# Value and phase projections in 128x32 tiles instead of 128x64, with a planner whose durations, restart and weights are set anew

## The reference

```python
for l in range(6):                                  # batch 4, 512 tokens, window of 126 keys
    q, k, v = x @ Wq.T + bq, keys @ Wk.T + bk, keys @ Wv.T + bv     # keys: a zero row, then x
    o = softmax(mask(q k.T / sqrt(8))) v @ Wo.T + bo                # 16 heads of 8
    x = ln(x + o);  x = ln(x + gelu(x @ W1.T) @ W2.T)               # 512 hidden
# block 2: token-shift mix: sigmoid(xr Wr) * (relu(xk Wk)^2 Wv)
# block 3: causal attention, with a gate for each head and key:
ph = x @ w_phase;  phase = arctan2(ph[..., 0], ph[..., 1])
gate = lock * exp((cos(phase - carrier) - 1) / bandwidth) + (1 - lock)
attn = softmax(causal(q k.T / sqrt(8) + log(gate + 1e-6)));  y = (attn v) @ wo
# block 4: a router picks 3 of 8 experts for each batch row; tanh-gelu feed-forward of 512 in each
```

## Time and profile before

| | us |
|---|---|
| median of 3 runs | 1088.59 |
| lowest, highest | 1084.31, 1092.73 |
| the profiled execution's own time | 1091.71 |
| its span in the trace | 1089.9 |
| PE busy in it | 992.6 (91%) |
| DVE, ACT, POOL busy | 803.6, 743.7, 394.4 |

### The profile page before, as it was taken

How to read it: one execution, slowest core, us unless ns; L and a number is a source line. 1 busy time by engine, 2 the same in 40 slices (tenths; PEclk the granted TensorE clock), 3 DMA queues, 4 the chain that set the end, 5 groups by cost and what they waited for, 6 DMA issues and landing times. The chain is left out here.

```text
span 1089.9 us, 47233 instructions
## 1 busy us (share of the span) xinstructions
PE 992.6 (91%) x20024; PEld 698.8 (64%) x20024; DVE 803.6 (74%) x2420; ACT 743.7 (68%) x1399; POOL 394.4 (36%) x528
## 2 busy tenths in 40 slices
PE   3689999999999999999998999999978988899996
PEld 2366767777766777777765776776656544455674
DVE  6877778777777788777788666768888889882321
ACT  6266766677767766766773777667767787888653
POOL 8311444332324443333344214324556364401211
PEclk9789999999999999999998999999999999999998
DMA  6721231322234221323224122112020311410220
GB/s 187 132 42 44 61 62 47 87 42 57 63 62 106 62 51 42 87 55 62 62 61 98 26 47 62 37 28 72 3 61 10 54 36 29 120 41 23 68 69 20
DMA packets 72626, 64.80 MB, mean 59 GB/s; under 512 B 16226, under 2 KB 66914, under 8 KB 72418
## 3 DMA queue, kind: packets, MB, share of 16 engines
q1 hardware_dynamic: 71554, 60.99, 23.9%
q10 hardware_dynamic: 864, 0.79, 0.4%
HBM read 15.70 MB, written 1.05 MB: 15 GB/s over the span
## 5 line engine op out<-in xcount | busy, mean ns | idle before, releaser
L1053 ACT ACTIVATE probs<-b 128x443 f32<-128x443 f32 (+2 forms) x736 | 356.5, 544 | 137.1 <-PE b L788 92.6
L1258 DVE TENSOR_REDUCE mx<-b 128x2 f32<-128x378 f32 (+1 forms) x768 | 351.8, 508 | 118.8 <-PE b L741 117.4
L708 PE MATMUL b<-band,identb 64*64 64x252 bf16 x2304 | 170.3, 285 | 18.1 <-DVE mx L1258 8.8
L807 PE MATMUL b<-probs,vals 128*32 128x189 f32 (+5 forms) x3968 | 177.3, 310 | 2.6 <-DVE mx L1255 1.3
L807 PEld LDWEIGHTS b<-probs,vals 128*32 128x32 f32 x3968 | 109.9, 110 | 53.2 <-issue 14.1
L788 PE MATMUL b<-qpack,kpack 64*64 64x189 bf16 (+5 forms) x3968 | 138.5, 235 | 4.4 <-issue 4.2
L1582 POOL TENSOR_SCALAR veps<-mv 128x4 f32<-128x4 f32 x48 | 11.0, 230 | 353.9 <-DVE mv L1364 353.6
L741 PE MATMUL b<-kpack,qpack 62*64 62x189 bf16 (+1 forms) x3072 | 123.9, 239 | 0.7 <-issue 0.7
L708 PEld LDWEIGHTS b<-band,identb 64*64 64x64 bf16 x2304 | 66.9, 105 | 79.3 <-issue 32.9
L919 PE MATMUL b<-w,hid 128*128 128x128 f32 x768 | 109.2, 286 | 1.1 <-DVE mx L1258 0.6
L1255 DVE TENSOR_REDUCE mx<-b 128x1 f32<-128x512 f32 (+7 forms) x256 | 99.3, 445 | 9.0 <-PE b L756 8.6
(11 more groups left out here) (174 smaller groups left out, 1650.8 us busy)
## 6 DMA issues: line engine op xcount, KB each, us to landing
qpack<-qparts SPq DMA_DIRECT2D x168, 128.0 KB, 3.6
kpack<-kparts SPq DMA_DIRECT2D x162, 128.2 KB, 3.6
qpack<-mrows SPq DMA_DIRECT2D x224, 4.0 KB
w<-in_w SPq DMA_DIRECT2D x12, 256.0 KB, 4.3
w<-in_wa SPq DMA_DIRECT2D x12, 256.0 KB, 2.8
w<-in_wb SPq DMA_DIRECT2D x12, 256.0 KB, 3.1
rowt<-in_rowt SPq DMA_DIRECT2D x6, 384.0 KB, 3.4
stream<-in_x SPq DMA_DIRECT2D x4, 256.0 KB, 4.4
```

Of the source, the lines that this page charges most:

```text
L708: pe.matmul(out, identb[rows, rows], rhs.unsqueeze(1).to_broadcast([64, 2, 2, EDGE]), start=True, stop=False, skip_group_check=True)
L807: mm = pe.matmul(bank("sum", u, group)[32 * j:32 * j + 32, q0:q0 + w - skip], vals[:, u % 2, at:at + 32], probs[:, n % SETS, j, col + skip ...
L1053: act.activation(probs[:, n % SETS, j, 0:width], bank("exp", u, v, b)[:, 0:width], ACT.Exp, scale=SCALE).then_inc(a_emptied, 1)
L1258: red = dve.tensor_reduce(out[:, 2 * tb:2 * tb + 2], read[:, 0:2 * width].rearrange("p (t k) -> p t k", k=width), AX.X, ALU.max)
```

## The change

The value and the phase projections are cut into 32 tokens to a weight load: each chunk has four matmuls in place of two. Together they compute the same numbers into the same places of the same banks. Moving columns stay at 64 (values) and 2 (phases).

The planner is changed in five ways. The mode 128x64 is gone, and `v` and `phase` count as 128x32, the mode of `weigh`. The assumed durations are set anew, some down (`gelu`, `egelu`, `take`), some up (`phase`, `pack`, `rest`, `root`). A job that follows one of its own kind on its line (`queued`) no longer waits `SAME` for it. A PE job starts no earlier than `RESTART` = 170 ns after its last input or bank is there. And `TURN_WORTH`, `TABLE_WORTH`, `SLACK`, `BIAS` and `LATE` have other values, so that the order of all work on every engine may be another.

```diff
-WIDE, HALF, QUARTER, STRIPE = "128x128", "128x64", "64x64", "128x32"
+WIDE, QUARTER, STRIPE = "128x128", "64x64", "128x32"
-        ... "weigh": 165, "v": 200, "phase": 200}
+        ... "weigh": 139, "v": 200, "phase": 200}
+RESTART = 170
-FETCH, FETCHED, VLOADS = 3850, 256, 80
-TURN_WORTH = 827
-TABLE_WORTH = 188731
-SLACK = {"act": 323, "dve": 0, "pe": 23, "pool": 472, "sp": 953}
+FETCH, FETCHED, VLOADS = 3850, 256, 144
+TURN_WORTH = 209713
+TABLE_WORTH = 738617
+SLACK = {"act": 233, "dve": 10, "pe": 19, "pool": 0, "sp": 12503}
...
+        self.jobs[name].queued = self.jobs[behind] if behind is not None and behind[0] == name[0] else None
...
     def lead(self, source, job):
+        if source is job.queued:
+            return 0
...
+            if e == "pe":
+                at = max(at, job.ready + RESTART)
...
-        add("pe", ("phase", u), 200, [state, ("later",)], takes=[("phase", u)], mode=HALF, line="phase")
-        add("dve", ("take", u), 2762, ...
+        add("pe", ("phase", u), 900, [state, ("later",)], takes=[("phase", u)], mode=STRIPE, line="phase")
+        add("dve", ("take", u), 1900, ...
-                add("act", ("gelu", u, f), 590, ...
+                add("act", ("gelu", u, f), 460, ...
-            add("act", ("egelu", b, r, f), 500,
+            add("act", ("egelu", b, r, f), 340,
...
                 for c in range(NCHUNKS - 1):
-                    for h in range(2):
-                        mm = pe.matmul(bank("v", u)[64 * h:64 * h + 64, 64 * c:64 * c + 64],
-                                       state[:, u % BATCH, own + 64 * c:own + 64 * c + 64],
+                    for j in range(4):
+                        h, first = j // 2, own + 64 * c + 32 * (j % 2)
+                        mm = pe.matmul(bank("v", u)[32 * j:32 * j + 32, 64 * c:64 * c + 64],
+                                       state[:, u % BATCH, first:first + 32],
                                        wv[:, weights_of(u), 64 * h:64 * h + 64], start=True, stop=True)
...
                 for c in range(C8):
-                    for h in range(2):
-                        mm = pe.matmul(out[64 * h:64 * h + 64, 2 * c:2 * c + 2],
-                                       state[:, u % BATCH, 1 + 64 * c:65 + 64 * c], w_phase[:, :],
+                    for j in range(4):
+                        first = 1 + 64 * c + 32 * (j % 2)
+                        mm = pe.matmul(out[32 * j:32 * j + 32, 2 * c:2 * c + 2],
+                                       state[:, u % BATCH, first:first + 32], w_phase[:, :],
```

More of the change, by code:

```diff
@@ L100 @@
 TURN = {"q": 200, "k": 200, "out": 205, "hid": 200, "ffn": 200, "mixin": 200, "mixv": 200, "ehid": 200, "eout": 200,
-        "cat": 152, "turn": 152, "norm": 152, "rows": 152, "weigh": 165, "v": 200, "phase": 200}
+        "cat": 152, "turn": 152, "norm": 152, "rows": 152, "weigh": 139, "v": 200, "phase": 200}
 TURN_LEAST, TABLE_LOAD = 122, 1400
-FETCH, FETCHED, VLOADS = 3850, 256, 80
-TURN_WORTH = 827
-TABLE_WORTH = 188731
-SLACK = {"act": 323, "dve": 0, "pe": 23, "pool": 472, "sp": 953}
-BIAS = {"active": 244399, "add": -561621, "band": -186382, "blank": -112807, "bo": -453915, "bo_in": 585915, "cat":
-        626734, "cnorm": -805202, "consts": 165407, "even": -155481, "exp": -955897, "ffn": -2325414, "gelu":
-        -257190, "heads": -43296, "hid": 423046, "high": 372670, "ident": 870698, "in": -573901, "k": 15405,
-        "kclean": -2829616, "later": 92784, "load": -61978, "lower": -360033, "masks": -167087, "max": 3452,
-        "maxrows": 20310, "mrows": -824339, "norm": 583361, "ocat": 1789041, "odd": 745241, "out": -572133, "pack":
-        19261, "parts": -1284482, "place": -1397698, "q": 632237, "qclean": 23531, "recip": -148003, "residue":
-        54128, "rest": 606044, "root": 4162, "row": -208237, "scale": 711602, "score": 697, "shifts": -538280,
-        "sin": 5155, "split": -230018, "stats": 93602, "sum": 2099526, "top": -660846, "turn": 1328575, "v": 3226,
-        "weigh": -4423258, "x": 206705}
@@ new lines @@
+FETCH, FETCHED, VLOADS = 3850, 256, 144
+TURN_WORTH = 209713
+TABLE_WORTH = 738617
+SLACK = {"act": 233, "dve": 10, "pe": 19, "pool": 0, "sp": 12503}
+BIAS = {"active": -585703, "add": 231755, "band": 35505, "blank": -28124, "bo": -352909, "bo_in": -91319, "cat":
+        289335, "cnorm": -1050122, "consts": 293876, "even": -2032881, "exp": -1588749, "ffn": -1223054, "gelu":
+        94663, "heads": -651982, "hid": 1966161, "ident": -400538, "in": -58459, "k": -11609, "kclean": -872265,
+        "later": 426143, "load": -24827, "lower": 363808, "masks": 110964, "max": 225377, "maxrows": -170061,
+        "mrows": 128567, "norm": 2790856, "ocat": 252455, "odd": -818861, "out": 16306, "pack": -652638, "parts":
+        267703, "place": -44542, "places": 62763, "q": 296727, "qclean": -43417, "recip": -1217700, "residue":
+        -567425, "rest": 811447, "root": -14897, "row": 128924, "scale": 434446, "score": 1065271, "sin": -434129,
+        "split": -132149, "stats": 1285932, "sum": 49054, "top": -1243083, "turn": 861881, "v": 25920, "weigh":
+        -7392628, "x": 625594}
@@ new lines @@
+LATE = {"cat": -499461, "chosen": -1424153, "cout": -505336, "eadd": 1117368, "egelu": -493636, "ehid": -3459642,
+        "eout": -2315234, "exp": -304612, "expert": 229477, "gate": 315005, "gated": -5461910, "gates": -358739,
+        "heads": 179321, "k": 709410, "logits": -28803, "max": -902344, "maxrows": -448832, "mix": 787298, "mixed":
+        6877, "mixv": 2083221, "mrows": -307932, "nadd": 150452, "nroot": 327896, "nscale": -410382, "nstats":
+        -1903514, "ocat": 814457, "open": 379462, "out": 75705, "parts": 6172, "phase": 1008097, "q": 152873,
+        "recip": 280820, "rexp": -486724, "router": 1521171, "rows": -408723, "score": -256641, "scored": -9963,
+        "split": 410198, "spread": 62660, "square": 378964, "state": 595207, "store": 11715, "sum": -269602, "take":
+        1511972, "tanh": -183989, "top": 1020813, "turn": -57200, "v": 275631, "weigh": -989274, "weight": 55240,
+        "window": 3337}
@@ L167, in add @@
         after = [a for a in after if a is not None]
+        behind = self.last.get(line)
         if line is not None:
-            if line in self.last:
-                after.append(self.last[line])
+            if behind is not None:
+                after.append(behind)
             self.last[line] = name
@@ L237, in arrange @@
                     job.start = at
+                    ready = soon[name]
+                    for pool in {self.pool_of(k) for k in job.takes}:
+                        n = sum(self.pool_of(k) == pool for k in job.takes)
+                        ready = max(ready, self.free[pool][n - 1][0]) if len(self.free[pool]) >= n else ready
+                    job.ready = ready
                     if best is None or at < best[0]:
```

56 lines of the change are left out of this document (24 added, 32 removed).

## The result

| | before | after |
|---|---|---|
| median, us | 1090.66 (4 runs) | 1105.36 (4 runs, 1101.28 to 1106.51) |
| ratio to the kernel before, 95% interval | 1 | 1.0129 [1.0100, 1.0158] |
| own time of the profiled execution, us | 1091.71 | 1105.65 |
| its span, us | 1089.9 | 1103.9 |

The change makes the kernel 1.3% slower. I had forecast 1078.5 with a range to 1099 and given slower 0.15.

What follows compares the result with a forecast made beforehand. The prediction took TensorE's sequence of jobs as the bound (matmul in flight for 992.6 of 1089.9 us): 1091.7 - 2.3 (tiles) - 7.8 (order) = 1081.6 us profiled, 1078.5 on the scale of the medians; range 1061 to 1099.

Steps and rivals of the forecast that it cites:

- Rounds of the value projection: In `v` on TensorE, 18 rounds a windowed job fall from 58 to 56 ns: 1.0 us less over 28 jobs.
- Rounds of the phase projection: In `phase` on TensorE, 32-column weight loads halve the round to 29 ns: 1.9 us less.
- Turns: Mode changes on TensorE: 16 of 32 `v` and `phase` jobs, straight behind a `weigh`, save 0.18 each: 2.9 us less.
- Instructions: TensorE's instruction stream: twice the records in `v`, one job in ten held up by late instructions: 3.5 us more.
- The sum of the tiles: Value and phase projections on TensorE: -1.0 - 1.9 - 2.9 + 3.5 = -2.3 us.
- The order: New order on all engines saves 10% of TensorE's 52 us idle time and 3% of mode changes: -7.8 us.
- no air: Rival: TensorE waits at the weigh and the maxima, sent too close to their inputs; 1092 to 1110 us; chance 0.17.
- What would show it: Expected in the profile: TensorE's idle time from 100 to 950 us down some 5 us, issue waits 9 to 12.
- my three signs: Forecast wrong if TensorE's idle time moves over 10 us, issue exceeds 15 us, or a value projection takes 2 us.

Runs made afterwards that it cites:

- tiles_alone: The kernel before, order untouched, with the 32-token loads in values and phases: 1091.1 us, 1.0013 to the kernel before.
- order_alone: The changed kernel's planner and order with the old 64-token loads in values and phases: 1097.94 us, 1.0067 to the kernel before.
- moved_port: Kernel before with 32-token loads, its order refitted by small moves to a restart-free clock in which GpSimd instructions delay VectorE's: 1075.39 us, 0.9863.
- moved_port_2: moved_port found from another start of the random moves, same clock: 1073.34 us, 0.9855 to the kernel before.
- pool_alone: moved_exact with only GpSimd's queue reordered, the other engines' orders the same: 1068.03 us, 0.9808 to the kernel before.
- moved_port_restart: moved_port found again with the change's `RESTART` of 170 ns added to the clock: 1079.63 us, 0.9931 to the kernel before.
- moved_exact: Kernel before with 32-token loads, its order refitted by small moves to a clock without restart or any GpSimd rule: 1103.5 us, 1.0106.

## Why the prediction was wrong

**Rounds of the value projection: right.** From the first to the last record a windowed `v` takes 993 ns in place of 1047 and the next job follows as before, 54 ns less a job; I had 36. These are the groups and the timeline beside the earlier trace rows:

```profile
L851 PE MATMUL b<-wv,state 128*32 128x64 f32 x1792 | 31.7, 220 | 5.6 <-issue 5.6
...
L871 PE MATMUL b<-w_phase,state 128*32 128x2 f32 x256 | 2.9, 173 | 0.3 <-ACT state L1163 0.3
```

```profile
447.95 1.07 PE L819 MATMUL b<-probs,vals 128*32 128x189 f32 x24
448.84 1.07 PE L851 MATMUL b<-wv,state 128*32 128x64 f32 x64
449.73 0.29 PE L859 MATMUL b<-wv,state 128*32 128x64 f32 x8
449.96 0.30 PE L720 MATMUL b<-band,identb 64*64 64x252 bf16 x4
```

**Rounds of the phase projection: right.** 64 records take 533 to 574 ns and 0.10 to 0.12 to the next job, beside 1.03 us in the earlier trace rows; 35 ns a round where I took 29, so 1.5 us of the 1.9 forecast.

```profile
856.72 0.71 PE L871 MATMUL b<-w_phase,state 128*32 128x2 f32 x64
857.37 1.55 PE L834 MATMUL b<-state,wqk 128*128 128x512 f32 x3
```

The records of a `v` start 14 ns apart (72 in 993 ns). The Trainium skill (TensorE: Matmul & The Clock Gate, "Wait — 56ns, not 53.3ns?") has a floor of about 25 ns from start to start; for four tiles side by side the trace doesn't agree with it.

**Turns: wrong.** I read the 0.18 us behind a `weigh` in the earlier trace rows as the price of a change of mode, and took 16 of them off. In the old order nothing of it went: in 15 of the 16 places two semaphore instructions fill that time with either tile. The account of tiles_alone has 5.2 us less in turns, but 3.7 of them come back under "other", at these same places, and most of the rest under the lower clock. A change of mode by itself is 0.11. In the new order a `v` does start 12 to 90 ns after the last record of the `weigh` in seven of eight cases, but with 0.11 saved a job that is under 1 us. And I expected more than 16 of the 32 jobs beside a `weigh`, and the new order has 9 (eight `v`, one phase).

**Instructions: right in kind, wrong in place.** 169 loads, as forecast, and the waits that name issue rose from 9.0 to 12.9 us, where I had 12. But I spread 3.5 us over all `v`, on the old order's spacing. In the old order stops inside of four `v` and one phase cost 2.9 us, and stops elsewhere fell by as much, so that issue stayed (14.6 and 14.3). In the new order it is 5 us more than before and 13 more than the same order with the old tiles, since that order puts eight of the `v` in pairs. A job alone can be hit too (0.6 us in the `v` at 548.1 of tiles_alone); two in a row are 288 instructions in 2.2 us, and always meet a boundary that comes every 256.

**The sum of the tiles: mis-sized.** I had -2.3 us; tiles_alone measured +1.4 [-0.4, +3.3]. The rounds gave 3.0 where I had 2.9, the turns nothing where I had 2.9, and the issue stops stayed, where I had 3.5 more; that makes about -3. The other 4 to 5 us stay open. The lower clock took 5.2 us more in that one profile, but over all runs the mean granted clock is 0.976 with either tile.

**The order: the step that failed.** I took -7.8 us, 10% of the idle time and 3% of the turns, since the old durations were wrong by rows of the trace; order_alone measured +7.3 [+4.6, +10.0]. With these 15 us and the 9 of the tiles in the new order (+7 in place of -2.3) most of the distance from 1078.5 to 1105.4 is told; 2 more are the kernel before, 1090.66 here. The durations were wrong, but the argument from there to a better order doesn't hold. A better clock did find orders 1.4 to 1.9% faster (moved_port, moved_port_2, pool_alone), so there was more to gain than I had thought; it had to be right in the terms that decide. I had counted `RESTART` as a protection against stops. It was a term to doubt: the traces show 55 ns from VectorE's end to TensorE's start, it charges 170 on top of 155, and in moved_port_restart it made an order 0.7% slower. That it did so in the changed kernel isn't shown.

**The rival "no air" has the right time and the wrong place.** Its range, 1092 to 1110, holds 1105. But stops for ACT went from 39.5 to 38.3 us and for VectorE from 49.8 to 50.7. What came was a DMA that GpSimd's queue had held back, the missing instructions, and small waits between like jobs. So its bet, which bore 0.17, was won by other things.

**What would show it.** TensorE's idle time from 100 to 950 us rose by 9.5 us (52.2 to 61.7), where I had it fall by 5; by my bound of 10 that alone would not have counted as wrong, nor would issue (12.9, bound 15) or the `v` (1.14 us). None of my three signs was tripped, since 8.8 of the 14 us came while TensorE counts as busy, and I had given no sign for that.

What stays open: the changed kernel has only 7 slow `ztok` (4.1 us of excess; 5 and 2.5 before), so the lock doesn't explain its loss against the kernel before. How the 7 us of its order divide between the restart, the other figures and the new weights isn't known. A kernel with the new figures and the old weights (old_weights) has no time: in its order a write of `diff` on VectorE isn't held back until the read before it is done. The planner's own clock put that order 5.9% behind the changed one. The account names the stops, and only those in the pairs were removed by an experiment without bringing others of their size.

## What to carry to other kernels

What two changes cost need not add up: the tile that doubles the instructions made no measurable difference in two orders and cost 7 us in the third, where pairs of its jobs stand in a row and lose up to 2.3 us each, so time a tile in the order in which it will run. A gap at a change of mode need not be the price of the change: look for semaphore instructions in it before taking it off. A planner's clock is to be checked by replaying it over two orders that were timed on the chip; if it ranks them wrongly, look in the traces for durations that depend on what the neighbour engine does, before fitting again. And an engine that is 36% busy can hold the critical path through a lock: look at the slowest tenth of a group's instructions, not at its mean.

## What the runs showed of the hardware

- VectorE's float32 128x128 `TENSOR_SCALAR` from SBUF to SBUF takes 0.34 us alone and up to 1.45 us beside a GpSimd tensor instruction of 1.27 us; all 33 slow ones of moved_exact overlap one, and the 139 that overlap none are not slow; nor are 20 that overlap one, 12 of them an instruction on 128x4 elements.
- TensorE waits for instructions at one place of every 256, the same in nearly all cases (193, counted from the first; 89 of 99 stops), and 128 more instructions ahead move the stops to other jobs. The closest two loads of that queue were 3.68 us apart in the trace of before and 3.50 in that of after.
- Four tiles of 128x32 start float32 records 14 ns apart at 64 moving columns and 9 ns apart at two columns (543 ns for 64 records).
- Between a `weigh` and a `v` two semaphore instructions, with nothing left to wait for, take as long with a change of mode (268 to 271 ns from the last start to the next, kernel before) as without one (267 to 270, tiles_alone); without them it is 200 to 203 ns with the change and 90 without.
- After the stop of 3.3 us in moved_exact the granted clock of the next 4 us was 0.57: 3.4 of them at the level of 1.2 GHz, the rest at 2.4.
